# Two cross-attention layers on one core: keys in three groups, a mask load of its own, first queries stacked by ScalarE's queue, and new instruction orders

## The reference

```python
# layer 0 (the last 4 context tokens are prompts, with weights of their own)
q = heads(x @ W_q); k_t = heads(text @ W_k); v_t = heads(text @ W_v)
probs_t = softmax(q k_t^T * Dh**-0.5);  text_out = probs_t v_t
k_ip = heads(ip @ W_k_ip); v_ip = heads(ip @ W_v_ip)
sem = l2norm(probs_t text) . l2norm(ip)
probs_ip = softmax(q k_ip^T * Dh**-0.5 + 0.5 * sem) * spatial_mask
x = (text_out + probs_ip v_ip) @ W_out + b_out + x
# layer 1
q = heads(x @ Wq.T); k, v from all 64 tokens (77 wanted, 64 there, so the prompt part is empty)
x = softmax(q k^T / sqrt(D)) v @ Wo.T + bo + x
```

## Time and profile before

| | us |
|---|---|
| runs | 445.45, 442.94, 445.0 (median 445.0) |
| profiled execution, its time | 443.75 |
| profiled execution, its span | 441.9 |
| granted TensorE clock, mean | 0.985 |
| PE busy | 397.1 (90% of the span) |
| DVE busy | 292.1 (66%) |
| ACT, POOL busy | 221.2, 192.8 |
| chain that ended last | PE 25%, DVE 25%, POOL 15%, DMA 14%, SP's queue 8% |

### The profile page before, as it was taken

How to read it: one execution, slowest core, us unless ns; L and a number is a source line. 1 busy time by engine, 2 the same in 40 slices (tenths; PEclk the granted TensorE clock), 3 DMA queues, 4 the chain that set the end, 5 groups by cost and what they waited for, 6 DMA issues and landing times.

```text
span 441.9 us, 13510 instructions
## 1 busy us (share of the span) xinstructions
PE 397.1 (90%) x5172; PEld 240.4 (54%) x5172; DVE 292.1 (66%) x817; ACT 221.2 (50%) x489; POOL 192.8 (44%) x480
## 2 busy tenths in 40 slices
PE   6996979899999999999899867989999899998985
PEld 3454444555655665556555534554666566555643
DVE  3334827776778777967887774776776667666723
ACT  2341414554645545454455443456776676565651
POOL 5030303566666765656567648474442352211000
PEclk9898989999999999999999999899999999999999
DMA  8575371603606125052052037252652734637052
GB/s 210 130 102 112 85 90 27 115 4 98 90 12 117 17 68 74 4 116 48 6 114 26 3 54 88 67 78 65 74 118 52 110 83 56 115 63 102 4 168 74
DMA packets 27881, 33.57 MB, mean 76 GB/s; under 512 B 5733, under 2 KB 17193, under 8 KB 27817
## 3 DMA queue, kind: packets, MB, share of 16 engines
q1 hardware_dynamic: 26949, 31.31, 39.9%
q10 hardware_dynamic: 868, 1.39, 1.1%
HBM read 5.82 MB, written 2.62 MB: 19 GB/s over the span
## 4 chain that ended last, share of the span: by engine, by line
PE 25%; DVE 25%; POOL 15%; DMA 14%; SPq 8%; issue 8%; ACT 4%; DVEq 0%; POOLq 0%
DVE mx L1189 9%; PE ps L676 8%; POOL e L1342 7%; DVE wt L1156 6%; DMA qs<-qp 6%; DMA qs<-mt 4%; SPq L660 4%; PE ps L753 4%; PE ps L783 3%; SPq L651 3%; PE ps L859 2%; DMA wt<-in_WKIP 2%; POOL e L1349 2%; PE ps L825 2%; DMA ks<-kp 2%
## 5 line engine op out<-in xcount | busy, mean ns | idle before, releaser
L1085 ACT ACTIVATE pt<-ps 128x512 f32<-128x512 f32 x160 | 88.4, 595 | 69.3 <-PE ps L783 68.7
L1189 DVE TENSOR_REDUCE mx<-ps 128x8 f32<-128x480 f32 (+3 forms) x192 | 105.1, 578 | 11.2 <-PE ps L753 11.1
L825 PE MATMUL ps<-pt,gram 64*32 64x256 f32 x1280 | 86.5, 387 | 1.6 <-ACT pt L1085 1.5
L831 PE MATMUL ps<-pt,vb 64*32 64x256 f32 x640 | 85.6, 388 | 0.0
L802 PE MATMUL ps<-wt,cst 64*32 64x256 f32 x640 | 85.3, 388 | 0.0
L532 POOL TENSOR_TENSOR qp<-qr,qp 80x512 bf16<-80x512 f32 x28 | 32.4, 1157 | 77.3 <-ACT qp L1068 77.3
L753 PE MATMUL ps<-ks,qs 96*128 96x128 bf16 x640 | 54.8, 223 | 8.4 <-DMA ks<-kp 2.9
L783 PE MATMUL ps<-qs,ks 101*128 101x256 bf16 x320 | 52.4, 276 | 8.3 <-DMA qs<-mt 5.2
L1156 DVE TENSOR_TENSOR wt<-ps,pt 128x512 f32<-128x512 f32 x80 | 54.5, 681 | 4.9 <-PE ps L825 4.9
L753 PEld LDWEIGHTS ps<-ks,qs 96*128 96x128 bf16 x640 | 40.8, 99 | 30.4 <-issue 12.2
L1145 DVE TENSOR_TENSOR qr<-ps,qp 80x512 f32<-80x512 f32 x32 | 21.8, 683 | 41.7 <-ACT qp L1064 41.5
(11 more groups left out here) (112 smaller groups left out, 708.6 us busy)
## 6 DMA issues: line engine op xcount, KB each, us to landing
qs<-qp SPq DMA_DIRECT2D x96, 160.0 KB, 5.0
ks<-kp SPq DMA_DIRECT2D x96, 80.0 KB, 2.8
xa<-in_xT SPq DMA_DIRECT2D x8, 160.0 KB, 2.7
out_T<-xa SPq DMA_DIRECT2D x7, 160.0 KB, 2.2
ca<-in_ctxT ACTq DMA_DIRECT2D x2, 512.0 KB, 7.2
xa<-in_xT SPq DMA_DIRECT2D x8, 96.0 KB, 3.0
out_T<-xa SPq DMA_DIRECT2D x7, 96.0 KB, 2.3
qs<-mt SPq DMA_DIRECT2D x32, 20.0 KB
```

Source lines behind the costliest of these rows:

```text
L825: last = nc.tensor.matmul(ps[T * hh + 32 * m:T * hh + 32 * m + 32, bank, sub * S:(sub + 1) * S], gram[keys_of(hh), g % V_RING, 32 * m:32 * ...
L831: nc.tensor.matmul(region(pair, hh), stationary(g, pair, keys_of(hh)), pt[keys_of(hh), (5 * g + c) % P_RING, sub, :], start=(c in (0, 3)), ...
L1085: nc.scalar.activation(pt[:, (5 * g + c) % P_RING, :, :].rearrange("p a b -> p (a b)"), ps[:, 2 + (g + c) % 2, :], ACT.Exp, scale=SCALE).t ...
L1189: nc.vector.tensor_reduce(mx[:, tile, p0:p0 + np_, :], o[:, :, :, 0:nt], AX_X, ALU.max).then_inc(red_done, 1)
```

## The change

- The keys of layer 0 are projected in three groups, of batches 0 to 3, 4 to 7 and 8 to 15 (`KEYS`), rather than two of eight. The context is loaded in the same groups, the three loads one behind the other on ACT's queue without a wait between them.
- The key mask has a load of its own (`khm`, 80 x 4), so `kmask` 0 no longer waits for the constants.
- SP's loads have another order: prompt key weights, mask, `wqa`, then `x`. Of the remaining channels of `x` (`xb`) and of `wqb` only the part of the first pair is loaded at the start, by ACT; the other three parts of each are a new stage `xr` of SP (six DMAs, behind `q` 1).
- `q` 1 stands before `setup` on PE, in another bank than `q` 0.
- The columns of batch 0 in `qs` are stacked by six DMAs of 80 KB from ACT's queue (stage `qf`), and `sc` 0 waits for these (`q_first`). SP's `qd` 1 stacks only the columns of batch 1.
- The orders of all engines and the banks are new.

```diff
+SETUP = 16
+KEYS = (range(0, 4), range(4, 8), range(8, B))
...
                 if g == 0:
-                    eng.wait_ge(w_in, 16)
+                    eng.wait_ge(mask_in, 16)
                     eng.wait_ge(setup_sb, 4)
...
+            sp.dma_start(wkip[:, :, :], WKIP).then_inc(kv_in[0], 16)
+            sp.dma_start(khm[:, :], consts[0:HC, C_KHH:C_KHH + 4]).then_inc(mask_in, 16)
+            load_wq(0, x_in[0])
             load_pair(0, x_in[0])
-            load_wq(0, x_in[0])
-            sp.dma_start(wkip[:, :, :], WKIP).then_inc(kv_in[0], 16)
+            sp.dma_start(wk[1][:, :, :], WK[1]).then_inc(rest_in, 16)
             sp.dma_start(cst[:, :], consts).then_inc(w_in, 16)
...
+            def load_rest(g, _):
+                sp.wait_ge(q_ps, 2)
+                for part in range(1, 4):
+                    rows = slice(REST * part, REST * part + REST)
+                    sp.dma_start(xb[rows, 0, :], rest_of_x(xT, 0)[part]).then_inc(xb_in[1], 16)
+                    sp.dma_start(wqb[0][rows, part, :], WQ[0, 128 - HC:HC, 1]).then_inc(wqb_in, 16)
...
                     for j in [j for j, p in enumerate(Q_PARTS) if p == part]:
-                        sp.dma_start(qs[16 * j:16 * j + 16, slot, :, :], qp[:, g // 2 % 2, part]).then_inc(q_stacked[slot], 16)
+                        cols = slice(S if g == 1 else 0, 2 * S)
+                        sp.dma_start(qs[16 * j:16 * j + 16, slot, :, cols], qp[:, g // 2 % 2, part, :, cols]
+                                     ).then_inc(q_stacked[slot], 16)
...
-            project_keys(0, 0)
+            project_keys(0, KEYS[0], 0)
             pe.wait_ge(kv_in[0], 16)
-            project_prompts(wkip, 6, 0, 8)
+            project_prompts(wkip, 6, 0, KEYS[1][0])
...
                 pe.wait_ge(c_in[1], 16)
-                project_keys(0, 1)
-                pe.wait_ge(setup_sb, 4)
-                project_prompts(wkip, 6, 8, B)
+                project_keys(0, KEYS[1], 1)
+                pe.wait_ge(c_in[2], 16)
+                pe.wait_ge(setup_sb, 2)
+                project_keys(0, KEYS[2], 0)
+                project_prompts(wkip, 7, KEYS[1][0], B, 192)
...
                 if f == 0:
-                    pe.wait_ge(q_stacked[slot], 16 * len(Q_PARTS) * (g // 4 + 1))
+                    if g == 0:
+                        pe.wait_ge(q_first, 16 * len(Q_PARTS))
+                    else:
+                        pe.wait_ge(q_stacked[slot], 16 * len(Q_PARTS) * (g // 4 + 1))
...
+            for n, own in enumerate(KEYS):
+                cols = slice(own[0] * T, (own[-1] + 1) * T)
+                if n == 2:
+                    act.wait_ge(xb_zeroed, 1)
+                    act.dma_start(xb[0:REST, 0, :], rest_of_x(xT, 0)[0]).then_inc(xb_in[0], 16)
+                    act.wait_ge(wqb_zeroed[0], 1)
+                    act.dma_start(wqb[0][0:REST, 0, :], WQ[0, 128 - HC:HC, 1]).then_inc(x_in[0], 16)
                 act.dma_start(ca[:, :, cols], ctxT[:, :, cols]).then_inc(c_in[n], 16)
...
+            def qf(g, part):
+                act.wait_ge((q_h, q_m, q_l)[part], 2)
+                for j in [j for j, p in enumerate(Q_PARTS) if p == part]:
+                    act.dma_start(qs[16 * j:16 * j + 16, 0, :, 0:S], qp[:, 0, part, :, 0:S]).then_inc(q_first, 16)
```

More of the change, by code:

```diff
@@ L393, in xattn_kernel @@
         fside = sb("fside", [128, 2])
+        khm = sb("khm", [HC, 4])
         xa = sb("xa", [128, ROWS])
@@ L430, in xattn_kernel @@
         w_in, rest_in, late_in, late1_in = sem("w_in"), sem("rest_in"), sem("late_in"), sem("late1_in")
-        c_in, kv_in = [sem(f"c_in{n}") for n in range(2)], [sem(f"kv_in{n}") for n in range(2)]
+        mask_in, wqb_in, xb_zeroed, q_first = (sem(n) for n in ("mask_in", "wqb_in", "xb_zeroed", "q_first"))
+        c_in, kv_in = [sem(f"c_in{n}") for n in range(3)], [sem(f"kv_in{n}") for n in range(2)]
         x_in = [sem(f"x_in{n}") for n in range(B // 2)]
@@ L452, in xattn_kernel @@
         yr_ps, yr_sb, padded = sem("yr_ps"), sem("yr_sb"), sem("padded")
-        xb_in, wqb_zeroed = ([sem(f"{p}{n}") for n in range(2)] for p in ("xb_in", "wqb_zeroed"))
+        xb_in, wqb_zeroed = [sem(f"xb_in{n}") for n in range(3)], [sem(f"wqb_zeroed{n}") for n in range(2)]
         ident = cst[:, C_ID:C_ID + 128]
@@ L982, in _ @@
             nc.scalar.preload_act_table_set("natural_log_exp_and_others")
-            for n in range(2):
-                cols = slice(n * 8 * T, (n + 1) * 8 * T)
-                need(act, c_in[0], 32 * n)
-                act.dma_start(ca[:, :, cols], ctxT[:, :, cols]).then_inc(c_in[n], 16)
-                if n == 0:
-                    act.dma_start(xb[:, 0, :], rest_of_x(xT, 0)).then_inc(xb_in[0], 16)
-                    act.wait_ge(wqb_zeroed[0], 1)
-                    for part in range(4):
-                        rows = slice(REST * part, REST * part + REST)
-                        act.dma_start(wqb[0][rows, part, :], WQ[0, 128 - HC:HC, 1]).then_inc(x_in[0], 16)
@@ L994, in keep_keys @@
-            def keep_keys(layer, n, first):
+            for n, own in enumerate(KEYS):
[5 more added lines that the diff above has]
+                    act.dma_start(wqb[0][0:REST, 0, :], WQ[0, 128 - HC:HC, 1]).then_inc(x_in[0], 16)
+                act.dma_start(ca[:, :, cols], ctxT[:, :, cols]).then_inc(c_in[n], 16)
@@ L996, in keep_keys @@
+            def keep_keys(layer, own, n, first):
                 for half in range(2):
                     act.wait_ge(setup_ps, first + half)
-                    nc.scalar.copy(kt[layer][:, half, 8 * n:8 * n + 8, 0:NT[layer]],
-                                   ps[0:HC, 2 + 2 * half + n, :].rearrange("p (b t) -> p b t", t=T)[:, :, 0:NT[layer]]
+                    nc.scalar.copy(kt[layer][:, half, own[0]:own[-1] + 1, 0:NT[layer]],
+                                   ps[0:HC, 2 + 2 * half + n, 0:len(own) * T].rearrange("p (b t) -> p b t", t=T)[:, :, 0:NT[layer]]
@@ L1000, in keep_keys, with keep_prompts @@
                                    ).then_inc(setup_sb, 1)
-            def keep_prompts(n, first):
+            def keep_prompts(bank, b0, b1, col, first):
                 act.wait_ge(setup_ps, first + 1)
                 for half in range(2):
-                    nc.scalar.copy(kt[0][:, half, 8 * n:8 * n + 8, T - N_IP:],
-                                   ps[0:HC, 6, half * 64 + n * 32:half * 64 + n * 32 + 32].rearrange("p (b t) -> p b t", t=N_IP)
+                    c = col + half * 64
+                    nc.scalar.copy(kt[0][:, half, b0:b1, T - N_IP:],
+                                   ps[0:HC, bank, c + N_IP * b0:c + N_IP * b1].rearrange("p (b t) -> p b t", t=N_IP)
```

240 lines of the change are left out of this document (131 added, 109 removed), and 180 rows, old and new, of tables (BANK_MOVED, FILL_BANK, MOVED, PE_AT).

## The result

The changed kernel takes 434.05 us (median of 3 runs, 432.25 to 434.07) against 445.0 us (442.94 to 445.45): ratio 0.976, 95% interval 0.9721 to 0.9798. That is 10.95 us faster; I had said 2.6 us, 442.4, and a range from 437.6. On another chip it took 434.36 us (6 runs), ratio 0.9767 [0.973, 0.9805].

The account below looks back on a forecast made before the run. PE, busy 90% of the span, was taken to bound the kernel, with only the start loose. Start 1.3 + clock 0.5 + tail 0.8 = 2.6 us: profiled execution 441.15, median 442.4 against 445.0; range 437.6 to 446.7.

Parts of the forecast that it names:

- Keys of four batches first: Start of PE: first keys at half the context load, about 5.3 us; idle times of 1.43 and 1.84 us gone.
- X: Start of `q` 0 on PE: 12.78 us before, forecast 10.3, between 8.4 and 12.1 to 12.5.
- From X to the first scores: Start: PE ready at X + 22.15, queries landed at X + 22.8 and ending the wait; gain 1.3 us.
- S: Start of the first scores: 34.42 us before, forecast 33.1; a shift is carried to the end.
- I leave half clock over `q` 0: Start: PE idles 2.6 us before `q` 0, so it stays at clock 0.50, 3.42 us as before.
- The clock behind the first scores: Behind the first scores, `vk` 2 at half clock: a shorter PE wait wins 0.5 us (bounds 0 and 1.0).
- The tail: Kernel end: `zt2` before `y` 31 fills 0.46 us of idle PE, last rows start sooner; 0.8 us (bounds 0, 0.8).
- The new orders of steps 1 to 30: Behind the start: 9 us of idle PE in 160 is all there is; 0, with 2 us either way.
- `x` early: Rival, start: `x` lands early, X 8.4, full clock kept, S 29.5; gain 6.7 us, 438.3; chance 0.18.
- the rival's S of 36.8: Rival, first scores: both queues' stacks go down together (X + 26.5), 2.4 us later; 446.6, no change; chance 0.08.
- the halved stacks' price: Rival, query stacks: half-length pieces cost as much as whole, S 41.0, 6.6 us later, 450.8; chance 0.07.
- orders that cost: Rival, PE's full middle: new orders cost what the start wins, 2 to 3 us; 445; chance 0.12.

Follow-up runs that it names:

- e9: Changed kernel with the first queries' six half stacks issued from SP's queue instead of ACT's, second key stacks behind the first maxima: 436.43 us, ratio 0.9841.
- e18: Kernel before plus 15 passes of an unread constant in two idle stretches of PE (ahead of `st1.0` and of layer 1's first scores): 439.82 us, ratio 0.9906.
- e6: Changed kernel without `qf`: first queries stacked whole, six 160 KB DMAs from SP's queue ahead of the layer-1 loads: 437.91 us, ratio 0.987.
- e13: e10 with the stacks of queries 2 and 3 in halves too, one half from SP, the other from ACT: 431.91 us, ratio 0.9708.
- e7: Changed kernel with two PE tail stages put back: `zt` 29 behind `pv31.2`, `zt2` 31 behind `y` 31: 437.44 us, ratio 0.9835.
- e3: Kernel before with two PE tail stages moved: `zt` 29 ahead of `st31`'s scores, `zt2` ahead of `y` 31: 444.97 us, ratio 1.0014.
- e2: Kernel before with only the changed kernel's new places and banks behind the first scores, its start left as it was: 439.67 us, ratio 0.9899.
- e5: Kernel before with six single places of the new order around the step from layer 0 to layer 1: 445.07 us, ratio 1.0004.
- e1: Changed kernel's code and its places up to the first scores, all other places and banks those of before: 436.84 us, ratio 0.9839.
- e10: e9 plus ACT's `qh` 1, `qm` 1 ahead of `setup`, SP's key and query stacks ahead of `xr`, first `vk` between first scores: 434.6 us, ratio 0.9777.
- e14: e10 with step 1's maxima ahead of SP's stacks of queries 2 and 3, most of step 1 ahead of step 2's scores: 435.67 us, ratio 0.978.
- e12: Kernel before with first-block query columns stacked first by SP in six half DMAs, then the other halves in six more: 447.03 us, ratio 1.004.

## Why the prediction was wrong

The direction was right and most of the start's geometry too. The size was not: 2.6 us against 10.95. By the prediction's own steps:

- **Keys of four batches first, and X.** Right. Keys at 5.65 (5.3 was said), `q` 0 at 10.09 against 10.3. `x` landed 6.20 us after its last issue, between my 4.7 and 8.8.
- **From X to the first scores.** The queries ended the wait, 0.36 us behind PE, as said. With half clock over `q` 0 (the changed kernel run again) S is 32.60 against my 33.1, a gain of 1.8 us against my 1.3. At full clock it is 30.94. Failed step: "with X at 10.3 PE idles 2.6 us, so I leave half clock over `q` 0". PE idled 1.41 us and the clock stayed up; it falls there in some executions of either kernel, and I took one profile's state for a property of the code. The landing of the last half stack was right: 4.65 us, my 2.8 alone and 1.7 for sharing, with SP's `qd` 1 issued from 26.99 on, 0.74 us behind ACT's last. In e9, where SP issues the same halves itself and no other queue has stacks, the last took 2.94.
- **The clock behind the first scores.** 0.5 us for one spell, where the term should have been for all of them. The profile of before had four, its runs 3.6, the changed kernel's 1.8: 1.8 x 1.6 = 2.9 us of the 10.95. I had shown two of the four in the earlier trace rows and not looked for others. This is the largest missing term; e18 shows its price by itself. The one spell that the term was for is still there in the first profile (0.52 in 34 to 37 us), and from the first scores to the first exponential 0.2 us were won; in the second profile it is gone, and 1.5 were. What in the new start brings fewer is not settled: e6 and e9, with the stacks of the first queries issued by SP, have 3.4 to 3.5 again, which speaks for the halves on ACT's queue; but e13 has them on SP's queue too and 1.6 spells.
- **The tail.** Right mechanism, mis-sized: 0.8 predicted, 1.7 measured (e7, and the distance in e3). I priced the second copy only; the two copies now stand together and the 0.46 us of idle PE ahead of `y` 31 is gone as well.
- **"The new orders of steps 1 to 30: ... I take 0, with 2 us either way."** Failed. e2 has the new places alone and is 4.5 us faster: 1.9 in the tail, 1.8 at the layer boundary, 0.8 between steps 1 and 2 by its step times (its profile also starts 1.5 us earlier, without the spell over `q` 0, and loses 0.5 in the middle and 1.1 in layer 1). The 9 us of idle PE that I gave as all there is are those of 80 to 240 us. From 256 to 276 PE is busy 13.6 of 20 us, and it waits 2.86 us in one piece for the first key stack of layer 1 (windows and PE's timeline of the kernel before):

```profile
256.00:276.00 20.00, 13.62 (x215) 8.03 (x213) 11.37 (x32) 8.05 (x20) 11.79 (x32) 0.99 0.62 78
```

```profile
274.99 1.40 PE L753 MATMUL ps<-ks,qs 96*128 96x128 bf16 x16 [2.86 <-DMA ks<-kp]
```

In the middle, where I had looked, nothing was won: from step 2 to 14 0.6 us is lost. At the boundary SP issues those key stacks 12.7 us behind the first exponential of step 14, before 13.8, and the last lands 1.4 us sooner by the same measure. Which of the moved stages brings that was not found; e5 shows that six near ones do not (13.8 there too).

In the two profiles the 9.7 us of span come out so. X is 2.7 us earlier. From X to the first scores 1.6 are won by the spell over `q` 0 that the first profile of the changed kernel lacks, and 0.8 lost by the longer way. 0.6 come up to the first exponential of step 1. Of the 2.3 between steps 1 and 2, 1.5 are a spell (14.75 us before; 13.20 in e1, with the places of before and no spell there) and 0.8 the places (e2). The middle loses 0.6, the boundary wins 2.1 and the tail 1.7. So 3.1 us are spells, 4.6 places outside the first steps, and 1.9 the start's way, where I had 1.3.

The rivals: `x` early gave 438.3 for X 8.4, and X was 10.09; the stacks did share for their last part but not to the rival's S of 36.8, and the halved stacks' price (a whole stack 6.43 us, a half 4.65) and orders that cost did not come. At an equal number of spells (mean spans 443.2 for before, 435.6 for e1, 438.3 for e2, 432.7 for the changed kernel, less 1.6 for each spell of the table) the start is worth 4.9 us, the places 4.8, both 7.8. The 1.9 us by which they don't add are little more than six runs of each can tell (1.7 either way, an estimate from their scatter). Of e1's own profile, 4.8 us of span with one spell fewer, 1.6 are the boundary's, where its spell fell ahead of the wait.

## What to carry to other kernels

Look for idle stretches of the bounding engine over the whole span before a new order is priced at nothing: the middle, which is long, hid two short places that held 4 us. Compare the mean granted clock of several runs, not of one profile, and price a stretch at half clock as a term of its own, by what waits behind it: here 15 passes without effect were worth 4 us of 445. A first wait that is shortened only pays as far as the next DMA in the queue lets it: ahead of that wait, count what the issuing engine has queued.

## What the runs showed of the hardware

- The granted clock fell to 0.50 (1.2 GHz) at or behind idle stretches of PE of 0.6 to 3.0 us, for 3.4 us (6.8 in e6, e10 and e14). Some idle stretches of that length brought none (1.41 us ahead of `q` 0 in the changed kernel, 1.74 ahead of step 16's scores in e13), and the same code got it in some executions and not in others (first scores at 32.60 and 30.94 us).
- A spell costs what it delays: 1.7 and 1.6 us over `q` 0, 1.5 behind `st1.0`, 1.3 behind the wait at the layer boundary, 0 to 0.3 ahead of that wait (e1, e10, e12).
- A 20 KB DMA issued on an idle queue landed 6.65 us later while 960 KB issued by another engine's queue were under way, as late as behind them in the same queue (6.83 us); with no query stacks under way it took 2.45 us in the changed kernel.
- The steps of layer 1 differ by 1 to 2 us between executions of one kernel at full clock: the first exponential of step 20 at 320.17 us in one profile of the changed kernel and at 321.23 in the other, with step 19's 0.1 us apart. The DMA of the maxima between them was issued 0.25 us sooner in the second and landed in 3.71 us instead of 2.41, which is the 1.06 us. Each profile has one slow issue of SP ahead of it (1.63 us in the first, 1.47 in the second, the others 0.6), so that is not the cause; why the DMA took longer is open. The chain of waits, first and second profile:

```profile
317.29 2.41 DMA qs<-mt
```

```profile
317.04 3.71 DMA qs<-mt
```
